# Projections of a latent-attention block: row normalisation on ScalarE, and the rotary key in eight matmuls with one doubled weight block

## The reference, cut to what matters

```python
def _layernorm(x, axis=-1, eps=1e-05):
    m = jnp.mean(x, axis=axis, keepdims=True)
    v = jnp.var(x, axis=axis, keepdims=True)
    return (x - m) / jnp.sqrt(v + eps)
...
c_q = x @ W_DQ                       # 512 -> 128
Qc = (c_q @ W_UQ)                    # 128 -> 16 heads x 32
Qr = rope(c_q @ W_QR)                # 128 -> 16 heads x 16
c_kv = x @ W_DKV                     # 512 -> 128
Kc = (c_kv @ W_UK)
Kr = rope((x @ W_KR)[:, None, :, :]) # 512 -> 16, one for all heads
V = (c_kv @ W_UV)
```

## Time and profile before

| | |
|---|---|
| median of 3 runs | 3141.35 us (3137.93 to 3144.23) |
| the profiled execution, first to last instruction (its span) | 3136.1 us; no other time of this execution is given, and the median of the runs is 5.25 us above it |
| PE busy over the span | 3003.5 us, 96% |
| DVE, ACT, POOL busy | 83%, 42%, 24% |

### The profile page before, as it was taken

How to read it: one execution, slowest core, us unless ns; L and a number is a source line. 1 busy time by engine, 2 the same in 40 slices (tenths; PEclk the granted TensorE clock), 3 DMA queues, 4 the chain that set the end, 5 groups by cost and what they waited for, 6 DMA issues and landing times.

```text
span 3136.1 us, 65472 instructions
## 1 busy us (share of the span) xinstructions
PE 3003.5 (96%) x23204; PEld 2201.6 (70%) x23204; DVE 2609.9 (83%) x4257; ACT 1307.7 (42%) x1946; POOL 745.7 (24%) x664
## 2 busy tenths in 40 slices
PE   8999599999999999979999999999999999999999
PEld 6777444444444444458888888888888888888887
DVE  8999478888788788778888888888888888888886
ACT  4455277777777777742222222222222222222221
POOL 2433200000000000013333333333333333333332
PEclk9999799999999999989999999999999999999999
DMA  6888846656556556551111111111111011111110
GB/s 234 280 291 274 235 111 136 137 131 139 131 132 140 129 131 138 127 157 35 41 41 38 35 35 41 40 41 41 41 40 40 31 40 37 41 41 40 41 34 14
DMA packets 251213, 304.22 MB, mean 97 GB/s; under 512 B 25552, under 2 KB 158544, under 8 KB 251088
## 3 DMA queue, kind: packets, MB, share of 16 engines
q1 hardware_dynamic: 251088, 302.89, 35.4%
HBM read 190.35 MB, written 112.46 MB: 97 GB/s over the span
## 4 chain that ended last, share of the span: by engine, by line
PE 48%; DVE 7%; issue 2%; ACT 0%; DVEq 0%; DMA 0%; ACTq 0%; POOL 0%; SPq 0%
PE p_ring L1708 16%; PE p_ring L1736 14%; PE ps_od L1708 9%; PE ps_od L1688 5%; PE p_ring L1726 2%; DVE sb_fp_tmp L102 1%; PE p_ring L1716 1%; DVE sb_h_amax L88 1%; DVE sb_stage L1585 0%; DVE sb_xq L1566 0%; DVE sb_xq L1560 0%; DVE sb_wg_lo L1614 0%; DVE sb_xq L104 0%; DVE sb_x_amax L88 0%; DVE sb_stage L100 0%
## 5 line engine op out<-in xcount | busy, mean ns | idle before, releaser
L919 ACT ACTIVATE sb_probs<-scores 128x1024 f32<-128x1024 f32 (+3 forms) x768 | 590.2, 813 | 239.8 <-PE scores L1122 232.9
L991 DVE TENSOR_SCALAR sb_probs<-sb_probs 128x2048 f32<-128x2048 f32 (+3 forms) x320 | 289.2, 904 | 120.2 <-ACT sb_probs L919 120.0
L669 POOL TENSOR_TENSOR sb_at_in<-sb_at_in,sb_inv_in 128x512 f32<-128x512 f32 x64 | 85.9, 1342 | 1130.4 <-DMA sb_inv_in<-dinv 1129.9
L1137 PE MATMUL ps_od<-sb_probs,sb_v 128*32 128x512 f32 (+3 forms) x3072 | 328.1, 499 | 2.5 <-DVE sb_probs L983 1.7
L1122 PEld LDWEIGHTS scores<-sb_q_hi,sb_k_hi 32*128 32x128 f32 x1536 | 73.7, 182 | 330.2 <-ACT sb_probs L919 309.8
L1708 PE MATMUL p_ring<-sb_wg_hi,sb_xq_hi 128*128 128x512 f32 (+1 forms) x1024 | 294.3, 368 | 0.3 <-DVE sb_wd_lo L1614 0.3
L1412 POOL TENSOR_TENSOR sb_stage<-sb_stage,sb_h_inv 128x512 f32<-128x512 f32 (+1 forms) x192 | 210.7, 1097 | 347.5 <-DVE sb_h_inv L94 347.5
L1708 PE MATMUL p_ring<-sb_wg_lo,sb_xq_hi 128*128 128x512 f32 (+1 forms) x1024 | 289.9, 364 | 0.0
L1708 PE MATMUL p_ring<-sb_wg_hi,sb_xq_lo 128*128 128x512 f32 (+1 forms) x1024 | 289.5, 364 | 0.0
L1736 PE MATMUL p_ring<-sb_wd_hi,sb_ht_hi 128*128 128x512 f32 x693 | 275.7, 398 | 0.0
L1736 PE MATMUL p_ring<-sb_wd_hi,sb_ht_lo 128*128 128x512 f32 x693 | 270.3, 390 | 0.0
(11 more groups left out here) (193 smaller groups left out, 6632.7 us busy)
## 6 DMA issues: line engine op xcount, KB each, us to landing
kq<-sb_kq_out SPq DMA_DIRECT2D x32, 1024.0 KB, 6.3
sb_kq_raw<-kq SPq DMA_DIRECT2D x64, 512.0 KB, 8.5
sb_xin<-in_L_attn_x_dram SPq DMA_DIRECT2D x32, 512.0 KB, 5.5
rq<-sb_r_out SPq DMA_DIRECT2D x64, 256.0 KB, 2.9
v<-sb_v_out SPq DMA_DIRECT2D x64, 256.0 KB, 3.6
sb_qr<-rq SPq DMA_DIRECT2D x256, 64.0 KB
sb_kr_hi<-kr SPq DMA_DIRECT2D x32, 512.0 KB
sb_kr_lo<-kr SPq DMA_DIRECT2D x32, 512.0 KB
```

The source lines that it names most:

```text
L919: act.activation(probs[:, k % PROBS, 2 * pair:2 * pair + 2, off:BANK], scores[(2 * k + pair) % RING2][:, :, off:BANK], ACT.Exp, scale=SCAL ...
L991: i = dve.tensor_scalar(pr, pr, P_MAX, P_MIN, ALU.min, ALU.max)
L1137: mm = pe.matmul(ps_o[rows, off:BANK], v_sb[s][:, j, rows], probs[:, k % PROBS, i, off:BANK], start=(j == 0), stop=last)
```

## The change

Four things are done.

1. `normalise` moves from DVE to ACT. It is computed as `rstd * x + shift` in four ACT instructions. DVE makes `negmean` (the negated mean), POOL makes `shift = negmean * rstd` behind the power. On ACT it stands behind the cast of C1, and for the first body ahead of the first cast of the weights.
2. A KR weight block has both forms in it: columns 0 to 63 the rounded weights, 64 to 127 their rests (`kr_both`). Against the rounded x this gives hi x hi in partitions 0 to 47 and lo x hi in partitions 64 to 111. A second block (`kr_high`: the rounded weights, and zeros in 64 to 127) is used against the rest of x. That makes 4 x 2 = 8 matmuls.
3. ACT copies partitions 64 to 111 to `whole_kr` and DVE adds partitions 0 to 47; the rope products read `whole_kr`.
4. Before the first body, DVE copies the KR columns once more and builds the two forms of the blocks in two copies and a memset.

```diff
@@ gpsimd
-                pool.wait_ge(s_stat, m * 9 + 9)
+                pool.wait_ge(s_stat, m * 10 + 10)
+                if not (isinstance(m, int) and m == 0):
+                    pool.wait_ge(xin_free, m * 2)
                 pool.tensor_tensor(rstd[:], vareps[:], mhalf[:], ALU.pow).then_inc(s_rstd, 1)
+                own(pool, s_rstd, m * 2 + 2)
+                pool.tensor_tensor(shift[:], negmean[:], rstd[:], ALU.mult).then_inc(s_rstd, 1)
@@ scalar
+            def normalise(m):
+
+                act.wait_ge(s_rstd, m * 2 + 3)
+                for u in range(2):
+                    for s in range(2):
+                        j = 2 * u + s
+                        i = act.activation(xhat[:, u, s, :], xin[:, u, s, :], ACT.Identity, bias=shift[:, j:j + 1],
+                                           scale=rstd[:, j:j + 1])
+                        if s == 1:
+                            i.then_inc(xin_free, 1)
+
+            normalise(0)
             act.wait_ge(s_lat, 32)
             act.copy(w_hi[:, 0:O_KR], w_raw[:, 0:O_KR]).then_inc(s_whi, 1)
...
                         act.copy(c_hi[:, int(name[1])], ps[:, 0]).then_inc(act_hi, 1)
+                        if name == "C1" and not last:
+                            normalise(n + 1)
+                    elif name == "KR":
+                        act.wait_ge(ps_ready, number + 1)
+                        if not (isinstance(n, int) and n == 0):
+                            freed(act, n - 1, "KR")
+                        act.copy(whole_kr[:], ps[64:96 + DR, 0, :]).then_inc(kr_rest, 1)
@@ vector
+                if not (isinstance(m, int) and m == 0):
+                    dve.wait_ge(s_rstd, m * 2 + 1)
+                dve.tensor_scalar(negmean[:], moments[:, :, 0], -1.0, None, ALU.mult).then_inc(s_stat, 1)
                 dve.tensor_scalar(vareps[:], moments[:, :, 1], LN_EPS, None, ALU.add).then_inc(s_stat, 1)
-
-            def normalise(m):
-
-                dve.wait_ge(s_rstd, m + 2)
-                for u in range(2):
-                    for s in range(2):
-                        j = 2 * u + s
-                        i = dve.tensor_scalar(xhat[:, u, s, :], xin[:, u, s, :], moments[:, j, 0:1], rstd[:, j:j + 1],
-                                              ALU.subtract, ALU.mult)
-                        if s == 1:
-                            i.then_inc(xin_free, 1)
...
-            dve.memset(krw[:, :, 48:128], 0.0).then_inc(s_kr, 1)
+            dve.memset(krw[:, :, 48:64], 0.0).then_inc(s_kr, 1)
...
+            own(dve, s_kr, 8)
+            dve.tensor_copy(krw[:, :, 64:128], krw[:, :, 0:64]).then_inc(s_kr, 1)
...
             own(dve, s_wlo, 2)
+            kr_both = w_hi[:, O_KR:O_UQ].rearrange("p (c n) -> p c n", c=DC)
+            kr_high = w_lo[:, O_KR:O_UQ].rearrange("p (c n) -> p c n", c=DC)
+            dve.tensor_copy(kr_both[:, :, 64:128], kr_high[:, :, 64:128]).then_inc(s_wlo, 1)
+            dve.tensor_copy(kr_high[:, :, 0:64], kr_both[:, :, 0:64]).then_inc(s_wlo, 1)
+            own(dve, s_wlo, 4)
+            dve.memset(kr_high[:, :, 64:128].bitcast(F32), 0.0).then_inc(s_wlo, 1)
...
-                        if k == 1 and not last:
-                            normalise(n + 1)
...
-                        dve.tensor_tensor(turned_kr[:, 0, :], ps[0:DR, 0, :], rope[0:DR, 1, pos], ALU.mult)
-                        dve.tensor_tensor(turned_kr[:, 1, :], ps[32:32 + DR, 0, :], rope[32:32 + DR, 3, pos],
+                        dve.wait_ge(kr_rest, n + 1)
+                        dve.tensor_tensor(whole_kr[:], ps[0:32 + DR, 0, :], whole_kr[:], ALU.add).then_inc(kr_whole, 1)
+                        own(dve, kr_whole, n + 1)
+                        dve.tensor_tensor(turned_kr[:, 0, :], whole_kr[0:DR], rope[0:DR, 1, pos], ALU.mult)
+                        dve.tensor_tensor(turned_kr[:, 1, :], whole_kr[32:32 + DR], rope[32:32 + DR, 3, pos],
@@ tensor
-                        pe.wait_ge(s_wlo, 2)
-                        i = three(ps[:, 0, :], [(w(O_KR + c * P), xt[c]) for c in range(DC)])
+                        pe.wait_ge(s_wlo, 5)
+                        kr_both, kr_high = ([w(O_KR + c * P)[h] for c in range(DC)] for h in range(2))
+                        for c in range(DC):
+                            pe.matmul(ps[:, 0, :], kr_both[c], xt[c][0], start=(c == 0), stop=False)
+                            i = pe.matmul(ps[:, 0, :], kr_high[c], xt[c][1], start=False, stop=(c == DC - 1))
```

More of the change, by code:

```diff
@@ L142, in projections @@
         vareps = sb("vareps", [P, 4])
+        negmean = sb("negmean", [P, 4])
         rstd = sb("rstd", [P, 4])
+        shift = sb("shift", [P, 4])
         mhalf = sb("mhalf", [P, 4])
@@ L150, in projections @@
         turned_kr = sb("turned_kr", [DR, 2, BANK])
+        whole_kr = sb("whole_kr", [32 + DR, BANK])
         turned = sb("turned", [P, 2, 2, BANK])
@@ L179, in projections @@
         xt_done = sem("xt_done")
+        kr_rest = sem("kr_rest")
+        kr_whole = sem("kr_whole")
         rope_sum = sem("rope_sum")
@@ L342, in _ @@
                 round_x(u, u, u)
-            act.wait_ge(s_kr, 8)
+            act.wait_ge(s_kr, 9)
             act.copy(w_hi[:, O_KR:NW], w_raw[:, O_KR:NW]).then_inc(s_whi, 1)
@@ L386, in row_stats @@
                         dve.bn_stats(stats[:, 2 * u + s, :], xin[:, u, s, :]).then_inc(s_stat, 1)
-                own(dve, s_stat, m * 9 + 4)
+                own(dve, s_stat, m * 10 + 4)
                 dve.sem_inc(stats_seen, 1)
@@ L390, in row_stats @@
                     dve.bn_aggr(moments[:, j, :], stats[:, j, :]).then_inc(s_stat, 1)
-                own(dve, s_stat, m * 9 + 8)
+                own(dve, s_stat, m * 10 + 8)
+                if not (isinstance(m, int) and m == 0):
+                    dve.wait_ge(s_rstd, m * 2 + 1)
+                dve.tensor_scalar(negmean[:], moments[:, :, 0], -1.0, None, ALU.mult).then_inc(s_stat, 1)
                 dve.tensor_scalar(vareps[:], moments[:, :, 1], LN_EPS, None, ALU.add).then_inc(s_stat, 1)
-            def normalise(m):
-                dve.wait_ge(s_rstd, m + 2)
-                for u in range(2):
-                    for s in range(2):
-                        j = 2 * u + s
-                        i = dve.tensor_scalar(xhat[:, u, s, :], xin[:, u, s, :], moments[:, j, 0:1], rstd[:, j:j + 1],
-                                              ALU.subtract, ALU.mult)
-                        if s == 1:
-                            i.then_inc(xin_free, 1)
             def rest_of_x(u, where, hi_count, free_count):
@@ L417, in _ @@
             row_stats(0)
-            normalise(0)
             dve.wait_ge(s_whi, 1)
```

## The result

The changed kernel takes 3154.86 us (median of 5 runs, 3151.9 to 3156.8) against 3141.35 (5 runs, 3137.93 to 3145.98). The ratio is 1.0043, with a 95% interval from 1.0031 to 1.0056: slower by 13.5 us. The forecast was 3142.2, no measurable change. The time lies 0.14 us inside the upper edge of the range (3155) and outside the span of the likeliest case (3136 to 3148). It is near the rival with a dear step on ACT's path (3153.5).

What follows compares the result with a forecast made beforehand. A DVE, POOL, ACT, DVE loop of 21.10 us a body was taken as the bound, PE outside it. Bodies -0.6, start +1.9, last body -0.5 gave +0.8 us: 3142.2, range 3127 to 3155.

Steps and rivals of the forecast that it cites:

- rival with a dear step on ACT's path: POOL's `shift` costs 1.01 us like the power, moving ACT by 0.76 a body: 3153.5; chance 0.21 with dear ACT.
- ACT at 0.61: ACT's normalisations take 0.61 us each instead of 0.52, adding 5 us; shares the 0.21 chance with dear `shift`.
- the prediction's own signs of being wrong: `shift` near 1 us, ACT instructions over 0.6 us apart, no short DVE operation stretched, or PE's clock falling in waits.
- The loop: DVE, POOL, ACT, DVE close each 21.10 us body, without PE; M is the end of DVE's last product of R.
- `negmean`, the power, `shift`: Before ACT's normalisation: `negmean` adds 0.10 us, power takes 1.01, `shift` 0.25; ACT sees it at M+4.66.
- Four normalisations on ACT: On ACT behind C1's cast: four instructions 0.52 us apart, 2.08 in all, ending at M+6.74; upper bound 0.61 each.
- The copy of the rests and the add: ACT's copy 0.59 us, DVE's add 0.69 plus 0.04 wait; rope products start at M+8.11, against M+8.15 before.
- The clash: POOL's `kr_out` subtraction moves from L485 to L90: L90 loses about 1.07 us, L485 regains 1.05, net zero.
- The start: Before the first body: later weight casts, DVE's extra copies and memset, and the new normalisation path cost +1.9 us.
- The last body: PE's KR comes over 1 us earlier, DVE adds right after c_lo and begins the products at 341.94: -0.5 us.
- DVE's relief counts in full: Rival: DVE loses 2.1 us a body, PE becomes the bound at 19.26: 3116 us, chance 0.06.
- second table: Rival: ACT's function needs two table loads of 1.28 us in each of 15 bodies, +38 us: 3180, chance 0.06.

Runs made afterwards that it cites:

- experiment 1: Changed kernel with KR as before (twelve matmuls, no copy, no add), normalisation still on ACT: 3128.6 us, ratio 0.9957.
- experiment 4: Changed kernel with the copy of the KR rests on DVE: 3136.18 us; or with ACT's copy after two of the four normalisations: 3138.53 us.
- experiment 5: Kernel with only the normalisation on ACT, KR cut to eight matmuls by leaving out the pass with the weights' rests: 3125.81 us, ratio 0.9944.
- experiment 3: Changed kernel with constant scale, constant bias, or both in ACT's normalisation: 3146.19, 3145.04 and 3141.16 us.

## Why the prediction was right where it was, and where it failed

That the time lies inside the range is luck: it does so by 0.14 us, where the kernel's runs spread over 4.9 us and two of the five are above 3155. The range reached that far for other cases (a dear `shift`, or ACT at 0.61), and one of the prediction's own signs of being wrong came true: ACT's instructions follow each other by more than 0.6 us.

- **The loop.** Right. The body followed ACT's time one to one (0.73 us for 0.75), and PE's four matmuls bought nothing in it: eight against twelve is 0.05 us a body even with nothing paid for them. The sentence "of the 2.94 us, 2.00 become a wait and 0.74 the add" does not add up to its 0.04, because recorded times overlap; by starts and ends, DVE is free at M+5.37 and went on at M+8.15, 2.78 us, and 2.78 - 2.00 - 0.74 is 0.04.
- **`negmean`, the power, `shift`.** Right: ACT's first normalisation starts at M+4.77 (forecast M+4.66). `shift` is 0.20 us (0.25).
- **"Four normalisations on ACT".** This is the step that failed. It had 4 x 0.52 = 2.08 with 0.61 as the most that one could take; they took 2.96. I took the price from casts and copies, which read no value for each partition. Two such values cost 0.09 us each in each instruction, 0.75 us a body; of the other 0.13, 0.12 is that the copy does not overlap the last normalisation, which the forecast had let it do. The spacing without such values, 0.52, was right. The upper bound was no bound, because it was the duration of another kind of instruction.
- **The copy of the rests and the add.** Right: 0.58 and 0.72 (forecast 0.59 and 0.73). The rope products start at M+9.06 against the forecast M+8.11, and 0.88 of these 0.95 us are the step above.
- **The clash.** Right: L90 grew to 1.18 us, L485 (now L515) fell to 0.71. Moving POOL's subtraction away brought L90 back to 0.18. The Trainium skill's rule ("SBUF — State Buffer", section "SBUF: two separate sides"), that DVE and GpSimd share a pair of ports as an exclusive lock, agrees with the rows: POOL came first, and L90 ended 0.04 us behind it. In other variants the same subtraction fell on L94 (0.80), on L100 (1.41), or on the multiplication that makes `piece_big` behind L485 (1.40 in place of 0.43, in experiments 1, 4 and 5).
- **The start.** The first M is 3.9 us later, where the forecast had +1.9. One round of normalisation lies on its path, 0.88 longer. The rest is a wait that I had wrong: I let the body's normalisation start at 25.97, behind POOL's `shift`, but it starts at 27.27, 1.3 later, behind the cast of C1, and that waits for PE. PE begins C0 at 18.38 instead of 16.78: the weights' cast on ACT stands behind the first normalisation, and DVE's subtraction and rests of X stand behind that cast (the rests end at 18.27 instead of 16.67). I had 0.4 us for this. C0's twelve matmuls then took 5.3 us, where before they took 4.3. Rows of PE and ACT of the changed kernel, then the cast of C1 in the kernel before:

```profile
18.38 0.79 PE L546 MATMUL p_ring<-sb_xt_hi,sb_w_hi 128*128 128x512 f32 x1 [3.34 <-DVEq L435]
...
26.78 0.59 ACT L376 CAST sb_c_hi<-p_ring 128x512 fp32r<-128x512 f32 x1 [2.29 <-PE p_ring L546]
27.27 2.93 ACT L343 ACTIVATE sb_xhat<-sb_xin,sb_shift,sb_rstd 128x512 f32<-128x512 f32 x4
```

```profile
24.23 0.59 ACT L355 CAST sb_c_hi<-p_ring 128x512 fp32r<-128x512 f32 x1 [2.30 <-PE p_ring L516]
```

- **The last body.** +0.55 against -0.5. I had PE's KR over 1 us earlier than DVE could use it. It came later: ACT's copy waited for PE (1.28 us in the profile) and DVE for the copy (1.25). The length of ACT's normalisation in the body before decides it: without the two values (experiment 3) these waits are 0.48 and 0.36, and the last body takes 16.99 us, 0.36 less than before. It was this normalisation again, then, that held PE back.
- **The sum.** Of the 16.5 us by which the last M is later, the forecast had 0.8. By the same working with 2.96 in place of 2.08: -0.6 + 14 x 0.88 = 11.7 for the bodies (12.0 found) and 1.9 + 0.88 + 1.3 = 4.1 for the start (3.9 found), and the last body as above. The mispriced normalisation is 12.3 of the 15.7 us missed. In the medians the difference is 13.5.
- **The rivals.** `shift` was not dear; ACT's instructions were, by more than I allowed. "DVE's relief counts in full" is false for the whole change and nearly true for its first half: with KR left alone the body fell to 20.32, where PE without its wait of 0.91 would need 20.19 (an estimate, 21.10 - 0.91), and the kernel gained 0.43%. No second table was loaded in the bodies. PE's granted clock was 0.98 to 1.00 over the bodies (before 1.00), and PE is not in the loop.

By their ratios (of 3141.35 us) the two halves of the change give -13.5 and -1.9 us alone (the second within its interval of no difference) and +13.5 together. At the end of the stage, in the profiles, it is -8.5, +3.9 and +16.7. Shown is why: the KR half puts a copy on ACT, directly behind the instructions that the other half has moved there, and makes DVE wait for it. With that copy on DVE the body falls by 1.69 us.

## What to carry to other kernels

Before an operation is moved to an idle engine, look at what else in the change waits on that engine's queue: an engine that is 42% busy over the program (50% in this stage's bodies) can still be in the loop, and there its instruction counts in full. Price a moved instruction with the same kind of operands, not the same shape; here two values read for each partition were 0.75 us a body. A shorter matmul chain on PE is worth next to nothing where PE already waits, or where another engine's chain is as long (experiment 5). When a store is moved in SP's order, the loads behind it are moved too.

## What the runs showed of the hardware that was not expected

The feed-forward stage, whose code no kernel here touches, did not always take the same time. Its first POOL instruction, in experiment 1 and in the run with DVE's copy:

```profile
1351.73 0.10 POOL L1404 MEMSET sb_mhalf<- 128x1 f32 x1 [19.82 <-POOLq L698]
```

```profile
1350.34 0.10 POOL L1421 MEMSET sb_mhalf<- 128x1 f32 x1 [19.55 <-POOLq L715]
```

From there to the end of the spans (3126.9 and 3134.5) are 1775.2 and 1784.2 us. Attention had begun within 0.1 us in both (360.23 and 360.31). Over the profiles of this study it was 1774.6 to 1784.2 us (before 1778.7, after 1779.0); attention took 988.7 to 991.5. Between the two kernels shown the totals go with the kernel: the runs of experiment 1 lie within 0.8 us, those with DVE's copy within 5.1, and the two groups don't overlap. But the kernel before, unchanged, had runs from 3136.1 to 3147.8 us, so a good part can also differ from run to run, and only the profiled one shows its stages. In the longest profile PE waited six times for `sb_xq` in the middle of the stage, 4.4 us in all, up to 1.4; in experiment 1 it never did. That is half of the 9 us. What shifts it is not settled. It means that 9 us of the difference between two kernels of this program can come from a stage that neither changed, and that the gain of an edit in the first stage is better read at that stage's end.
